# Linear attention over a long context: the bent exponential of the keys moves from VectorE to ScalarE, one group ahead

## The reference, cut to what matters

```python
def _feature_map(x):
    return jnp.where(x > 0, x + 1.0, jnp.exp(x))
kvp = kv @ Wkv.T
k, v = jnp.split(kvp, 2, axis=-1)
k = _feature_map(k.reshape(B, S, H, hd).transpose(0, 2, 1, 3))
kv_summary = jnp.einsum('bhsd,bhse->bhde', k, v)
k_sum = k.sum(axis=-2)
z = 1.0 / (jnp.einsum('bhld,bhd->bhl', q, k_sum)[..., None] + EPS)
attn = jnp.einsum('bhld,bhde->bhle', q, kv_summary) * z
```

## Time and profile before

| | |
|---|---|
| median of 3 runs | 3083.01 us (3080.39 to 3083.06) |
| profiled execution | 3065.16 us, its span 3063.4 us |
| busy over the span | PE 2850.4 us (93%), DVE 2140.2, ACT 1698.2, POOL 1649.9 |
| the stage's exponentials (L490) | 192, the first at 67.7 us, the last at 728.7 us |

### The profile page before, as it was taken

The page is one execution under the profiler, slowest core; times in us unless marked ns, Lnnn a source line. Parts: engine busy times, 40 slices in busy tenths (PEclk is TensorE's granted clock), DMA queues, the critical chain, the costliest instruction groups (busy, mean ns, idle before and its releaser), DMA issues. The chain is left out here.

```text
span 3063.4 us, 59857 instructions
## 1 busy us (share of the span) xinstructions
PE 2850.4 (93%) x20910; PEld 2456.4 (80%) x20910; DVE 2140.2 (70%) x3314; ACT 1698.2 (55%) x3065; POOL 1649.9 (54%) x1795
## 2 busy tenths in 40 slices
PE   5999999998899927999999999999999999977999
PEld 3999999997556615888888888888888888866998
DVE  4888888886422253877778787777777778766554
ACT  2666666663212204667666666666666666652443
POOL 2888888885221104565556655566565555631322
PEclk9999999999899968999999999999999999997999
DMA  4544454453611121111101111011110111122000
GB/s 133 153 151 145 146 151 144 146 151 86 203 55 46 45 56 47 60 50 38 59 29 59 49 38 59 29 59 46 41 58 30 59 34 54 35 78 95 7 6 12
DMA packets 107280, 225.11 MB, mean 73 GB/s; under 512 B 32224, under 2 KB 80464, under 8 KB 102192
## 3 DMA queue, kind: packets, MB, share of 16 engines
q1 hardware_dynamic: 101888, 215.86, 23.0%
q0 software_dynamic: 3216, 8.29, 0.8%
q10 hardware_dynamic: 2112, 0.12, 0.1%
HBM read 193.24 MB, written 27.33 MB: 72 GB/s over the span
## 5 line engine op out<-in xcount | busy, mean ns | idle before, releaser
L1554 DVE TENSOR_TENSOR a_probT<-a_p,a_probT 125x448 fp32r<-125x448 f32 x768 | 458.8, 617 | 154.5 <-ACT a_probT L1487 151.5
L1487 ACT CAST a_probT<-a_p 125x448 fp32r<-125x448 f32 x768 | 395.6, 537 | 255.3 <-PE a_p L1671 254.4
L1548 DVE TENSOR_REDUCE a_mxs<-a_s 112x1 f32<-112x1500 f32 x256 | 439.7, 1717 | 97.8 <-PE a_s L1659 94.2
L1686 PE MATMUL a_o<-a_probT,a_val 125*64 125x224 f32 x3072 | 473.2, 277 | 1.7 <-DVE a_probT L1554 0.9
L1671 PE MATMUL a_p<-ident,a_prob 112*125 112x112 f32 x3072 | 438.6, 274 | 2.5 <-DVE a_probT L1554 2.3
L1671 PEld LDWEIGHTS a_p<-ident,a_prob 112*125 112x125 f32 x3072 | 387.7, 188 | 43.7 <-issue 26.7
L1480 ACT ACTIVATE a_prob<-a_s,a_mxs 112x1500 f32<-112x1500 f32 x256 | 389.5, 1522 | 15.9 <-DVE a_mxs L1548 14.8
L1686 PEld LDWEIGHTS a_o<-a_probT,a_val 125*64 125x64 f32 x3072 | 337.8, 136 | 38.0 <-issue 24.5
L442 POOL TENSOR_TENSOR l_rows_lo<-l_raw,l_rows_hi 125x512 fp32r<-125x512 f32 x192 | 273.4, 1424 | 105.8 <-ACT l_rows_hi L477 105.8
L1404 POOL TENSOR_TENSOR a_two<-a_picked 64x224 f32<-64x224 f32 x128 | 84.1, 657 | 434.7 <-DVE a_picked L1566 434.7
L445 POOL TENSOR_TENSOR l_phik_lo<-l_phif,l_phik_hi 125x512 fp32r<-125x512 f32 x192 | 297.2, 1548 | 11.9 <-ACT l_phik_hi L483 11.9
(11 more groups left out here) (305 smaller groups left out, 7333.1 us busy)
## 6 DMA issues: line engine op xcount, KB each, us to landing
l_rawT<-in_ctxT SPq DMA_DIRECT2D x32, 1500.0 KB, 6.2
a_rawT<-in_ctxT SPq DMA_DIRECT2D x32, 1500.0 KB, 6.2
l_raw<-in_ctx SPq DMA_DIRECT2D x32, 1344.0 KB
e_wall<-in_L_ffn_w_gate_up SPq DMA_DIRECT2D x8, 1024.0 KB, 14.5
W_hi<-w_out_hi SPq DMA_DIRECT2D x32, 192.0 KB, 2.4
W_lo<-w_out_lo SPq DMA_DIRECT2D x32, 192.0 KB, 2.4
l_raw<-in_ctx SPq DMA_DIRECT2D x32, 156.0 KB
e_xb<-sorted_x SPq DMA_DIRECT2D x35, 129.0 KB, 2.0
```

Of the source, the lines that this page charges most:

```text
L1487: act.copy(p_target(j, f, 0), p_source(i)).then_inc(p_hi[i], 1)
L1548: dve.tensor_reduce(mxs[:, j:j + 1], s_bank[0:TT, :, 0:GW], AX.XY, ALU.max, negate=True).then_inc(max_done, 1)
L1554: dve.tensor_tensor(p_target(j, f, 1), p_source(i), p_target(j, f, 0).bitcast(F32), ALU.subtract).then_inc(p_read[i], 1)
L1686: mm = pe.matmul(o_bank[0:2 * PW, at:at + 2 * TT], flat(val[:, ch, j, :, :]), flat(probT[j % 2][:, ch, :, :]), start=(ch == 0), stop=(ch = ...
```

## The change

ACT's one exponential becomes two instructions. The first (`negative`) stands where the exponential stood: it takes relu of the negated keys from PSUM into `l_expk` and counts `min_done`. The second (`exponential`) stands behind `rows.hi` of the iteration and ahead of `GT` and `phik.hi`: it waits for `min_done` and takes, in place, the exponential of the negated value, and counts `exp_done`. DVE's min and its wait are gone; DVE's `l_phif` waits for `exp_done`. Ahead of the loops, both are issued one after the other for the first group.

```diff
                     if not (last and g == NP - 1):
-                        exponential(b, g + 1, first)
+                        negative(b, g + 1, first)
...
                     act.copy(rows.hi[:, g * CP:(g + 1) * CP, 0:D], raw[u][:, g * CP:(g + 1) * CP, :]).then_inc(rows_hi, 1)
+                    if not (last and g == NP - 1):
+                        exponential(b, g + 1)
                     if g == 4 and not first:
                         act.wait_ge(gt_full, b)
...
-            def exponential(b, g, first):
+            def negative(b, g, first):
 
                 act.wait_ge(k_full, NP * b + g + 1)
                 if g >= 2 or not first:
                     act.wait_ge(phi_done, NP * b + g - 1)
-                act.activation(expk[:, g % 2, :], k_bank[g % 2][0:CH, :], ACT.Exp).then_inc(exp_done, 1)
+                act.activation(expk[:, g % 2, :], k_bank[g % 2][0:CH, :], ACT.Relu, scale=-1.0).then_inc(min_done, 1)
+
+            def exponential(b, g):
+                act.wait_ge(min_done, NP * b + g + 1)
+                act.activation(expk[:, g % 2, :], expk[:, g % 2, :], ACT.Exp, scale=-1.0).then_inc(exp_done, 1)
...
                 for g in range(NP):
-                    dve.wait_ge(exp_done, NP * b + g + 1)
-                    dve.tensor_scalar(expk[:, g % 2, :], expk[:, g % 2, :], 1.0, None, ALU.min).then_inc(min_done, 1)
                     if g + 2 < NP:
                         t_low(b, u, g + 2)
...
-                    dve.wait_ge(min_done, NP * b + g + 1)
+                    dve.wait_ge(exp_done, NP * b + g + 1)
```

More of the change, by code:

```diff
@@ L500, in _ @@
             t_copy(0, 0, 1)
-            exponential(0, 0, True)
+            negative(0, 0, True)
+            exponential(0, 0)
             batch(0, 0, 0, first=True)
```

## The result

The changed kernel takes 3126.28 us (median of 4 runs, 3122.54 to 3127.62), the kernel before 3083.03 (median of 4 runs, 3080.39 to 3083.67); the ratio is 1.0141, 95% interval 1.0129 to 1.0153, so the loss of 43 us is clear of the scatter. The forecast was 3126.

What follows compares the result with a forecast made beforehand. PE was taken as the bound: 19.66 us own work plus 1.24 waiting per batch. +1.34 us per batch gave +40 over 30 batches, +43 with the stage's start: 3083 + 43 = 3126 us, range 3080 to 3140.

Steps and rivals of the forecast that it cites:

- The sum per batch: Change in PE's batch of 20.90 us: 0.51 + 0.69 + 0.94 - 0.80 = +1.34 us, for 30 batches.
- GT: ACT's copy behind the new exponential comes later; from keys of group 5 to group 0, 4.25 becomes 4.76 us, +0.51.
- Keys of group 2: `t_low` misses POOL's turn, so `kv_copy` and `numden` come later; from keys of group 0, 6.59 becomes 7.28 us, +0.69.
- Keys of group 4: New PE wait for `l_phif` of group 2 behind late `t_low`; from keys of group 2, 5.80 becomes 6.74 us, +0.94.
- Keys of group 5: PE's wait for `l_phif` of group 3 goes with the min, in time by 0.28 us: -0.80 us per batch.
- The price of the second exponential: ACT's new exponential behind `rows.hi` takes a step of 0.51 us, between 0.49 and 0.61; ACT does not become the bound.

## Why the prediction was right

The sum per batch was +1.34 us. Measured from the first relu after two batches (109.95 us) to the last (772.0), the stage grew by 662.05 - 622.42 = 39.6 us against the same exponentials before (106.28 to 728.7), over 29.8 batches: 1.33 each. The batch shown is one of the shorter ones; the batches alternate between about 22.16 and 22.28 us. Step by step, from the timeline of PE shown above:

- *GT*: keys of group 5 to those of group 0 are 308.40 - 303.61 = 4.79; forecast 4.76. Shown alone by the kernel with `GT` first.
- *Keys of group 2*: 315.75 - 308.40 = 7.35; forecast 7.28. In the longer batches it is 338.05 - 330.57 = 7.48.
- *Keys of group 4*: 322.49 - 315.75 = 6.74; forecast 6.74. The waits at groups 2 and 4 rest on `t_low` missing POOL's turn, forecast by 0.24 us; it misses it by 0.25 in iteration 0 and 0.26 in iteration 2. The kernel with `t_copy` early takes both away, the one with half of `phik.lo` more than half of them.
- *Keys of group 5*: 303.61 - 300.33 = 3.28; forecast 3.46, and 4.26 before. This is the term that was mis-sized: the removed wait gave -0.98, not -0.80. I had PE ready where the idle time of 0.80 began on the timeline, which is where the profile draws the end of `gt`, 0.60 us after its start at 307.80 (line below). But with no wait between them the keys start 0.35 us after `gt` starts (303.26 and 303.61 in the change, 315.81 and 316.17 without the min), so PE stood ready some 0.25 us earlier than I read. `l_phif` of group 3 was in time as forecast, but by less: it ends at 302.66 + 0.68 = 303.34 in the change, and with the 0.15 that is 0.12 ahead of the keys, not 0.28. The same 0.25 is why the kernel without the min (0.25 x 30 = 7.5) gained 32 us and not 24, and why the one with the exponential behind `t_copy` came out at 3053 and not 3059.
- *The price of the second exponential*: its step is 0.53 us, I took 0.51. ACT has not become the bound, and no further table load came with the relus; the one that is there stands behind the first relu now, where it is not hidden: 69.2 - 67.3 = 1.9 us from the relu to the exponential, where I had counted 0.6 or less.

```profile
307.80 0.60 PE L618 MATMUL l_gt<-ident,l_G 128*128 128x128 f32 x4
```

Against the steps before (4.26, 4.25, 6.59 and 5.80) the four steps of the batch shown give -0.98 + 0.54 + 0.76 + 0.94 = +1.26, and those of a longer batch about 0.13 more, nearly all at the keys of group 2. So the path was as forecast, step by step, but the sum agrees to 0.01 us with some luck: the removed wait was worth 0.18 more than I put, the later `GT` and the keys of group 2 together cost 0.1 to 0.2 more, and the two misses cancel.

By the Trainium skill, "ScalarE: Activation LUTs", section "Rules for kernel authors", relu and min belong on VectorE. On the price of one instruction the rows agree (0.362 us for the min alone, 0.598 for the relu). For the time of this kernel the measurement differs: with relu and exponential on ACT in idle time it takes 3052.74 us, 29 less than with the min on DVE. The min took 0.362 to 1.531 us, by what POOL was doing; the exponential on ACT took 0.624 to 0.637 in all 192 instances.

One step came out, but its cause is not the one I gave alone. I credited the wait at the keys of group 5 to the removed min, and in the order before, taking the min away does end that wait (3.21). But in the change's order the kernel with the min kept shows 3.29 there too: once the keys of group 4 are late, the min of group 3 falls elsewhere between POOL's instructions and costs 0.41 in place of 1.52. In the change's order the min is worth 15 us, in the order before 32. That is why +36 us was expected of it and +15 measured. The parts of such a sum are not independent: a wait moved by one edit changes what another edit is worth.

In the two profiled executions the difference is 57 us, not 43. Some 44 of it lies between first and last relu. Most of the rest lies behind the stage: from the first `e_sil` to the first `a_prob` it is 413.8 us in the profiled execution before (781.6 to 1195.4), and 425.2 in that after (827.4 to 1252.6); in the seven experiments it is 425.3 to 430.8. So it is the profiled execution before that was short there, which fits its 18 us under the median. Of the 11.4 us, 9.7 are three idle stretches of PE in the profile after, between 890.7 and 908.3 us (0.77, 3.51 and 5.42), for which the profile shows nothing that PE waited for; at the same place in the profile before, PE runs through. What causes them is open.

## What to carry to other kernels

Before moving work to an engine with idle time, see what stands behind the new place in that engine's queue: here the same edit loses 43 us with the exponential ahead of `GT` and `t_copy`, and wins 29 with it behind them, where the engine waited anyway. Where two engines exclude each other, a shift of half a microsecond decides who goes first, and the loser pays what is left of the other's instruction (here 1.04 of 1.29 us); so write both times of readiness beside each other, counted from the event that both hang on.

## What the runs showed of the hardware

A DVE instruction that waits for the ports gets them at POOL's next change even where POOL has its own next instruction ready: a `t_low` that was ready 0.26 us before POOL's change goes first (305.45 and 305.71, with the exponential behind `t_copy`), and one that was ready 0.25 us after it waits 1.04 us for POOL's end (312.79, and 312.54 to 313.83, in the change). It ended 0.54 us after POOL in the kernels before, after and with half of `phik.lo`. The exponential from SBUF takes 0.634 us for 125x512, the relu from PSUM 0.598 (medians of 192).
